# Windowed attention in six layers: probabilities divided ahead of their transposes, P V with V as weights, other order of the steps

## The chip, the cores and the metric

The kernel runs on one core of a Trainium2 chip. The metric is the device time of one execution in microseconds (us); runs of the same kernel are compared by their median. The core has five engines that each work through an instruction stream of their own, in order, and wait for one another by semaphores: TensorE (PE: matmuls from SBUF into PSUM), VectorE (DVE), ScalarE (ACT), GpSimd (POOL), and SyncE (SP), which here issues all DMA transfers.

## What is computed

The input is 2048 tokens of 128 numbers. After a layer norm two branches are added to it. One is a small linear attention, done once at the start. The other, nearly all of the time, has six layers of

```
q, k, v = split(shift_tokens(x) @ Wqkv)            # 16 heads of 64
q, k    = l2norm(q) * q_scale, l2norm(k) * k_scale, then rotary (xPos)
sim     = 8 q k^T for windows of 32 queries x 64 keys (own window and the one before), masked
out     = softmax(sim) v
x       = out @ Wo + x
x       = (a * gelu(gate)) @ W2 + b2 + x           # a, gate = layernorm(shift_tokens(x)) * g + b, times W1, plus b1
```

all in float32.

## The kernel before

**Tiling.** A step is 256 tokens (`T`) of one layer, two chunks (`C`) of 128; eight steps (`G`) are a layer, so there are 48 (`N`). Work of a step has three stages: `a_` (projections, squares of the norms, rotary), `b_` (attention, first half of Wo), `c_` (second half of Wo, layer norm, feed-forward). In iteration `it` the kernel does stage `a` of step `it`, `b` of step `it-1` and `c` of step `it-2` (`LAG`).

**Order.** `SCHEDULE` (line 57) is one list of small parts, written out by hand or by a planner. `run` (line 72) goes through it once an iteration, and each engine picks out the parts that it has a function for. So the list gives each engine's order; between engines only semaphores count. PE's order before is: `a_v0 c_wo a_v1 c_mu b_rqt a_x0 a_y0 c_var b_s0 a_x1 a_y1 b_s1 a_norm0 a_norm1 c_h0 a_x2 b_pt0 b_att0 a_y2 b_pt1 c_h1 a_sp0 a_norm2 b_ot0 a_sp1 c_h2 b_att1 c_down a_x3 a_y3 b_wo b_ot1 a_norm3`. DVE's is: `b_rcq c_xb b_rq c_zc a_mx0 a_my0 c_zn b_scale0 a_mx1 b_max0 c_zl b_scale1 a_rck b_max1 a_my1 b_sum0 a_mx2 b_div0 c_hm0 a_my2 a_kn0 c_hm1 b_sum1 c_hm2 a_kn1 b_div1 c_fin a_mx3 a_my3 b_xb`. POOL's is `a_rot0 b_sub0 b_sub1 a_rl a_rot1 a_halo w_l0 c_wl a_xl+1 a_rot2 a_rot3 w_l1 w_l2`.

**The parts that matter here**, for a chunk `c` of step `n`:

- `b_s` (line 497): a mask matmul into PSUM banks 2 and 3, then 64 (72 in the first chunk) small products of 64 x 32 queries as weights and 64 keys streamed, one for each head and window, in a tile of 64 rows x 32 columns of the PE array. A float32 matmul is two records in the trace, each with its weight load.
- `b_scale` (DVE, 770): PSUM times the inverse norm of q into `E`. `b_max`, `b_sub` (POOL, 1097), `b_exp` (ACT): maximum, subtraction, exponential, all in `E` (128 x 1024). `b_sum` (784): sum and reciprocal `ri`.
- `b_pt` (529): eight PE transposes of `E` into banks 4 and 5; `b_pto` (ACT) copies them to `PT`.
- `b_att` (537): 64 products with 32 columns of `PT` as weights and 64 of V (`V2`) streamed, into banks 2 and 3. `b_div` (790, line 795) multiplies by `ri` into `On`. `b_ot` (556) transposes `On` by PE into banks 4 and 5, `b_oto` (ACT) copies that to `OT`, `out_proj` (564: `b_wo`, `c_wo`) multiplies by Wo.
- `a_x`, `a_y`: six matmuls each of the projections of k and q (`ps<-xh,wh` and the like); `a_v`: six of v. `a_mx`, `a_my` (line 716): two multiplications each by the rotary tables; `a_rot` (POOL, 1090) adds them; `a_kn` (759) scales k by its inverse norm, `a_sp` is the matmul that spreads that norm.
- `c_mu`, `c_zc`, `c_zsq`, `c_var`, `c_rs`, `c_zn` (825), `c_zh`, `c_zl` (830): the layer norm of the feed-forward; `c_h`, `c_gelu`, `c_hm` (837), `c_down`: its matmuls and gate. `c_h1` waits for `c_hm0`, `c_h2` for `c_hm1`.

**Transfers.** SP issues them in one fixed order a step: `windows` (16 transfers of V from `Vs` into `V2`, line 271), `keys` (8, line 294, after `a_kn1`), `queries` (8, line 306, after `a_rot3`), `halo` (2, line 285), and the rotary table of the next step. `b_s0` of a step waits for its keys and queries.

Line 353 is the helper `mm`, line 525 the transposes, line 863 the helper `act`.

## Time and profile before

| what | us |
|---|---|
| median of 3 runs | 2080.44 (2080.12 to 2084.45) |
| the profiled execution | 2084.09 |
| its span, first to last instruction | 2081.5 |
| PE busy | 1759.1 (85%) |
| DVE busy | 1416.7 (68%) |
| ACT busy | 1124.9 (54%) |
| POOL busy | 801.3 (38%) |
| mean granted clock of TensorE | 0.929 of full speed |

"Busy" counts the time in which at least one instruction of the engine runs; matmuls overlap one another, so a busy PE isn't necessarily at its peak, and the mean time of one record is longer than the distance between two. An idle time is put down to what ended it: "issue" means that the profile shows nothing that the engine waited for.

### The profile page before, as it was taken

To read this page: it belongs to the slowest core of one execution; us is meant where nothing else is said; L and a number is where in the kernel's file an instruction comes from. 1 tells how busy PE (TensorE), PEld (TensorE's weight loads), DVE (VectorE), ACT (ScalarE), POOL (GpSimd) and SP (SyncE) were. 2 spreads that over 40 slices of the span, in tenths; PEclk is the share of its full clock that TensorE was granted. 3 is DMA by queue.
4 is the path that set the end of the run, shared out by engine and by line. 5 is a ranking of instruction groups with operands and counts; after the bars stand their busy time and mean duration, and the time that the engine had idled before them with its cause. 6 is when DMAs were issued, how large, how long until landed. Compare 5 with 4: busy or idle time off the path is not lost.

```text
span 2081.5 us, 81277 instructions
## 1 busy us (share of the span) xinstructions
PE 1759.1 (85%) x35952; PEld 1447.0 (70%) x35952; DVE 1416.7 (68%) x2130; ACT 1124.9 (54%) x2065; POOL 801.3 (38%) x612
## 2 busy tenths in 40 slices
...
GB/s 92 0 185 108 133 144 101 103 155 157 108 144 126 93 133 176 117 129 138 100 124 154 144 105 132 134 93 133 120 156 105 124 145 113 107 127 141 111 127 23
DMA packets 98318, 252.96 MB, mean 122 GB/s; under 512 B 29872, under 2 KB 36144, under 8 KB 97200
## 3 DMA queue, kind: packets, MB, share of 16 engines
...
## 4 chain that ended last, share of the span: by engine, by line
PE 51%; SPq 22%; DVE 10%; issue 9%; DMA 3%; POOL 3%; ACT 2%; DVEq 0%; ACTq 0%
PE ps L353 45%; SPq L314 6%; SPq L278 6%; PE ps L525 6%; SPq L281 5%; DVE UV L716 4%; POOL Qtb L1090 3%; SPq L303 2%; DVE On L795 2%; DMA V<-Vs 1%; ACT PT L863 1%; SPq L291 1%; DMA Qtb<-Qtb 1%; SPq L283 1%; DVE sq L697 1%
## 5 line engine op out<-in xcount | busy, mean ns | idle before, releaser
L716 DVE SCALAR_TENSOR_TENSOR UV<-ps,veca,rope 128x512 f32<-128x512 f32 x768 | 527.3, 738 | 55.1 <-PE ps L353 29.7
L863 ACT ACTIVATE sq<-ps 128x512 f32<-128x512 f32 (+1 forms) x400 | 227.5, 582 | 354.9 <-PE ps L353 341.9
L1090 POOL TENSOR_TENSOR Kt<-UV 128x512 f32<-128x512 f32 x192 | 250.1, 1325 | 423.2 <-DVE UV L716 423.2
L1090 POOL TENSOR_TENSOR Qtb<-UV 128x512 f32<-128x512 f32 x192 | 241.9, 1283 | 252.6 <-DVE UV L716 252.5
L1100 POOL TENSOR_TENSOR E<-E,mx 128x1024 f32<-128x1024 f32 x96 | 190.2, 1982 | 319.4 <-DVE mx L782 319.4
L353 PE MATMUL ps<-Kb,Qtb 64*32 64x64 f32 (+1 forms) x12288 | 187.5, 236 | 87.9 <-issue 87.6
L353 PE MATMUL ps<-xh,wh 128*128 128x256 f32 x768 | 250.0, 326 | 12.3 <-ACT sq L863 4.2
L353 PEld LDWEIGHTS ps<-Kb,Qtb 64*32 64x32 f32 x12288 | 161.0, 112 | 121.8 <-issue 121.4
L353 PE MATMUL ps<-xh,wl 128*128 128x256 f32 x768 | 226.5, 295 | 4.1 <-issue 4.1
L353 PE MATMUL ps<-xl,wh 128*128 128x256 f32 x768 | 226.7, 295 | 2.3 <-issue 2.3
L353 PE MATMUL ps<-V,PT 64*32 64x64 f32 x12288 | 154.2, 229 | 48.3 <-issue 48.2
L776 DVE TENSOR_TENSOR E<-ps,rq 128x1024 f32<-128x1024 f32 x96 | 117.3, 1222 | 111.8 <-PE ps L353 111.6
L353 PE MATMUL ps<-OT,wo 128*128 128x128 f32 x1536 | 187.1, 275 | 0.6 <-issue 0.6
L353 PEld LDWEIGHTS ps<-OT,wo 128*128 128x128 f32 x1536 | 182.9, 192 | 5.5 <-issue 1.4
L353 PE MATMUL ps<-sq,ind 128*32 128x256 f32 x1536 | 169.0, 411 | 8.6 <-issue 7.3
L353 PEld LDWEIGHTS ps<-xh,wh 128*128 128x128 f32 x768 | 154.3, 201 | 26.0 <-issue 6.9
L353 PEld LDWEIGHTS ps<-V,PT 64*32 64x32 f32 x12288 | 132.1, 106 | 56.0 <-issue 53.7
L353 PEld LDWEIGHTS ps<-xh,wl 128*128 128x128 f32 x768 | 155.8, 203 | 7.1 <-issue 5.9
L863 ACT ACTIVATE E<-E 128x1024 f32<-128x1024 f32 x96 | 101.5, 1058 | 105.9 <-POOL E L1100 105.8
L353 PEld LDWEIGHTS ps<-xl,wh 128*128 128x128 f32 x768 | 156.1, 203 | 2.2 <-issue 2.2
L795 DVE TENSOR_TENSOR On<-ps,ri 128x1024 f32<-128x1024 f32 x96 | 116.8, 1217 | 57.3 <-issue 49.6
L863 ACT ACTIVATE hid<-ps,vecc 128x256 f32<-128x256 f32 x144 | 69.0, 479 | 139.8 <-PE ps L353 138.8
...
## 6 DMA issues: line engine op xcount, KB each, us to landing
...
```

The costliest lines, as they stand in the source:

```text
L278: e.dma_start(V2[r * DH + W:(r + 1) * DH, m % 2, C * w:C * w + C, :], Vs[w * W:(w + 1) * W, r, :, :]).then_inc(s["v2_in"], 16)
L281: e.dma_start(V2[r * DH:r * DH + W, m % 2, C * w + C:C * w + 2 * C, :], Vs[w * W:(w + 1) * W, r, :, :]).then_inc(s["v2_in"], 16)
L303: e.dma_start(Kb[p0:p0 + W, j0:j0 + HQ, :], Kt[hq * W:(hq + 1) * W, half, :, :]).then_inc(s["k_in"], 16)
L314: e.dma_start(Qb[p0:p0 + W, j0:j0 + HQ, :], Qt[hq * W:(hq + 1) * W, half, :, :]).then_inc(s["q_in"], 16)
L353: return e.matmul(out, lhsT, rhs, start=start, stop=stop, **kw)
L525: ins = e.transpose(ps[:, 4 + h // 4, (h % 4) * P:(h % 4 + 1) * P], src[:, h, :, :], ident[:, :])
L716: e.scalar_tensor_tensor(UV[:, p % 2, slot, :].rearrange("p (i t) -> p i t", i=2), ps[:, half, :].rearrange("p (i t) -> p i t", i=2), veca ...
L776: e.tensor_tensor(E[:, c].rearrange("p j r k -> p r j k"), ps[:, 2:4, :].rearrange("p r (j k) -> p r j k", k=KEYS), by_row.unsqueeze(3).br ...
L795: e.tensor_tensor(On[:, :, :, :].rearrange("p j r k -> p r j k"), ps[:, 2:4, :].rearrange("p r (j k) -> p r j k", k=DH), ri[:, c].rearrang ...
L863: return e.activation(out, in_, f, **kw)
L1090: e.tensor_tensor(dst, u, v, op).then_inc(s["rot_done"], 1)
L1100: e.tensor_tensor(ev, ev, mx[:, c].unsqueeze(2).broadcast_to([P, H, KEYS]), ALU.subtract).then_inc(s["sub_done"], 1)
```

## The change

Four things are changed.

1. The probabilities are divided by their sum ahead of the transposes: `b_div` (which read PSUM) goes, `b_nrm` multiplies `E` by `ri`, in SBUF, in place; `b_pt` waits for it.
2. P V is formed with V as weights (64 x 64) and 32 columns of `PT` streamed, in tiles of 64 x 64 of the array. The result comes out transposed as Wo needs it, so `b_ot` and `On` go; `b_oto` copies banks 2 and 3 to `OT`, and the host lays Wo out otherwise.
3. `b_s` and `b_att` become four parts each, of four head pairs. Centering in the layer norm is done by the matmul (`cen` = identity minus the mean), so `c_zc` goes, and `c_zsq` and `c_zn` read PSUM.
4. The list has another order, and waits for a layer's weights are made once a layer. `windows` now waits for the halo of the step before.

PE's order after is: `a_v0 a_v1 a_x0 a_y0 c_wo b_rqt a_x1 b_s0 b_s1 a_y1 c_mu c_var b_s2 b_s3 a_norm0 a_norm1 a_x2 a_y2 c_h0 b_pt0 c_h1 b_att0 a_norm2 c_h2 a_sp0 b_pt1 b_att1 a_sp1 c_down a_x3 a_y3 b_att2 b_wo b_att3 a_norm3`. DVE's is: `b_rcq a_mx0 a_my0 c_xb b_rq a_mx1 b_scale0 a_my1 b_max0 c_zn b_scale1 b_max1 a_rck c_zl b_sum0 b_nrm0 a_mx2 c_hm0 b_sum1 c_hm1 b_nrm1 a_my2 c_hm2 a_kn0 a_kn1 c_fin a_mx3 a_my3 b_xb`. POOL's is `a_xl+1 a_rot0 b_sub0 b_sub1 a_rot1 a_rl w_l0 a_rot2 w_l1 a_halo a_rot3 w_l2 c_wl`.

```diff
-SCHEDULE = """b_lnq b_rcq a_vs0 c_xs c_xb b_rq a_vs1 a_v0 c_zc a_rot0 c_zsq c_wo a_mx0 a_sqy0 a_v1 c_rs c_mu b_rqt a_x0
...
+SCHEDULE = """b_rcq a_v0 a_mx0 a_vs0 a_my0 a_v1 c_xb a_vs1 a_x0 b_lnq a_xs+1 a_y0 b_rq a_sqy0 a_sqx0 a_xh+1 c_xs c_wo a_xl+1
+    b_rqt w_h0 a_x1 a_mx1 a_rot0 a_sqy1 b_scale0 b_s0 b_sub0 c_zsq c_rs b_sub1 a_my1 b_max0 b_s1 a_y1 c_mu a_rot1
+    c_zh c_var a_sqx1 b_s2 b_s3 w_h1 c_zn b_exp0 b_scale1 a_rl w_l0 b_max1 a_rck a_lnk a_norm0 a_sqy2 b_exp1
+    a_norm1 a_x2 a_y2 c_h0 c_gelu0 b_pt0 c_zl a_rot2 c_h1 b_pto0 b_att0 a_sqx2 b_sum0 c_gelu1 a_rh a_norm2 c_h2
+    a_sp0 b_pt1 b_att1 c_gelu2 w_l1 a_sp1 b_nrm0 a_mx2 b_oto0 c_down c_hm0 a_halo a_rot3 b_sum1 c_hm1 b_nrm1 a_x3
+    b_pto1 a_my2 c_hm2 a_kn0 a_sqy3 c_wh a_y3 b_att2 a_sqx3 w_l2 a_kn1 c_fin b_wo a_mx3 b_att3 a_my3 a_norm3 c_wl
+    w_h2 b_xb b_oto1""".split()
...
@@ -271,6 +271,8 @@
             def windows(m):
 
                 e.wait_ge(s["vs_done"], m * 4 + 4)
+                if m:
+                    e.wait_ge(s["v2_halo"], m * 32)
...
@@ -494,21 +497,23 @@
-            def b_s(n, c):
-
-                if c == 0:
+            def b_s(n, i):
+
+                c, heads = i // 2, range(i % 2 * HQ, i % 2 * HQ + HQ)
+                chosen = 0 if n % G == 0 and c == 0 else 1
+                if i % 2 == 0:
+                    if i == 2:
+                        e.wait_ge(s["e_done"], n * C + c)
+                    elif n:
+                        e.wait_ge(s["ots_done"], n * 4)
+                    for r in range(2):
+                        if i == 0 and r == 1:
+                            e.wait_ge(s["k_in"], n * 128 + 128)
+                        mm(ps[:, 2 + r, :].rearrange("p (j k) -> p j k", j=HP), identb[:, :],
+                           mask[:, chosen:chosen + 1, :].broadcast_to([P, HP, KEYS]), True, False, skip_group_check=True)
+                if i == 0:
                     e.wait_ge(s["q_in"], n * 128 + 128)
...
             def b_pt(n, c):
-                e.wait_ge(s["p_done"], n * C + c + 1)
+                e.wait_ge(s["pn_done"], n * C + c + 1)
...
+            def b_att(n, i):
+
+                c, heads = i // 2, range(i % 2 * HQ, i % 2 * HQ + HQ)
+                if i == 0:
+                    e.wait_ge(s["e_done"], n * C + C)
+                elif i == 2:
+                    e.wait_ge(s["ots_done"], n * 4 + 2)
+                if i % 2 == 0:
+                    mm(ps[:, 2, 0:1], identb[:, :], identb[:, 0:1])
+                    e.wait_ge(s["pts_done"], n * 4 + 2 * c + 2)
+                for h in heads[::2]:
+                    for w in range(NW):
+                        for r, h in ((0, h), (1, h + 1), (0, h + 1), (1, h)):
+                            rows = slice(r * DH, (r + 1) * DH)
+                            ins = mm(ps[h % 2 * DH:(h % 2 + 1) * DH, 2 + r, h // 2 * P + w * W:h // 2 * P + (w + 1) * W],
+                                     V2[rows, n % 2, C * w + c, h * DH:(h + 1) * DH], PT[rows, h, w * W:(w + 1) * W],
+                                     tile_position=(r * DH, h % 2 * DH))
...
-                mm(ps[:, 2, 0:1], identb[:, :], identb[:, 0:1])
-                for h in range(HP):
-                    for r in range(2):
-                        for w in range(NW):
-                            rows = slice(r * DH, (r + 1) * DH)
-                            ins = mm(ps[w * W:(w + 1) * W, 2 + r, h * DH:(h + 1) * DH], PT[rows, h, w * W:(w + 1) * W],
-                                     V2[rows, n % 2, C * w + c, h * DH:(h + 1) * DH], tile_position=(r * DH, w * W))
-                ins.then_inc(s["o_done"], 1)
...
-                transposed(On[:, :, :, :], "ot_done")
...
             def c_mu(j, _):
                 e.wait_ge(s["z_act"], j * 2 + 2)
-                mm(ps[:, FF, 0:T], mean[:, :], zs[:, :]).then_inc(s["mu_done"], 1)
+                mm(ps[:, FF, 0:T], cen[:, :], zs[:, :]).then_inc(s["mu_done"], 1)
...
-            def b_div(n, c):
+            def b_nrm(n, c):
                 e.wait_ge(s["ri_done"], n * C + c + 1)
...
+                e.tensor_tensor(heads(E[:, c]), heads(E[:, c]), ri[:, c].unsqueeze(2).broadcast_to([P, H, KEYS]),
+                                ALU.mult).then_inc(s["pn_done"], 1)
...
-                e.scalar_tensor_tensor(zs[:, :], zs[:, :], vecc[:, j // G % 2, LG:LG + 1], zr[:, :], ALU.mult,
+                e.scalar_tensor_tensor(zs[:, :], ps[:, FF, 0:T], vecc[:, j // G % 2, LG:LG + 1], zr[:, :], ALU.mult,
...
-                    act(OT[:, 4 * i:4 * i + 4, :], ps[:, 4 + i, :]).then_inc(s["ots_done"], 1)
+                    act(OT[:, 4 * i:4 * i + 4, :], ps[:, 2 + i, :]).then_inc(s["ots_done"], 1)
...
-                act(zq[:, :], zs[:, :], ACT.Square).then_inc(s["zsq_done"], 1)
+                e.wait_ge(s["mu_done"], j + 1)
+                act(zq[:, :], ps[:, FF, 0:T], ACT.Square).then_inc(s["zsq_done"], 1)
```

## Rows read from the trace of the kernel before

**Rows 1.** The page, chain that ended last, by engine (q: its queue).
```profile
PE 51%; SPq 22%; DVE 10%; issue 9%; DMA 3%; POOL 3%; ACT 2%; DVEq 0%; ACTq 0%
```

**Rows 2.** Busy time and instructions by engine in the stretch of all steps.
```profile
core 0: us, PE busy (x) PEld busy (x) DVE busy (x) ACT busy (x) POOL busy (x), PEclk, DMA share, GB/s
143.00:2024.50 1881.50, 1639.07 (x34920) 1360.03 (x34920) 1301.55 (x1895) 1076.96 (x1972) 773.76 (x588) 0.95 0.55 127
```

**Rows 3.** Timeline of PE (start, us, engine, line, tiles, idle before): masks of `b_s0`.
```profile
143.03 0.99 PE L353 MATMUL ps<-mask,identb 128*128 128x512 bf16 x2 [2.83 <-DMA Qtb<-Qtb]
...
1552.23 0.61 PE L353 MATMUL ps<-mask,identb 128*128 128x512 bf16 x2 [1.01 <-DMA Qtb<-Qtb]
...
1588.75 0.59 PE L353 MATMUL ps<-mask,identb 128*128 128x512 bf16 x2
...
2024.54 1.03 PE L353 MATMUL ps<-mask,identb 128*128 128x512 bf16 x2 [1.28 <-DMA Qtb<-Qtb]
```

**Rows 4.** Timeline of SP's queue: keys and queries of one step.
```profile
1574.66 6.13 SPq L303 DMA_DIRECT2D Kb<-Kt  x8
1581.88 4.96 SPq L314 DMA_DIRECT2D Qtb<-Qtb  x8
```

**Rows 5.** Timeline of DVE in that step: `b_scale1`, `c_hm0`, `a_kn1`.
```profile
1559.45 1.23 DVE L776 TENSOR_TENSOR E<-ps,rq 128x1024 f32<-128x1024 f32 x1 [0.58 <-PE ps L353]
...
1567.15 0.47 DVE L837 SCALAR_TENSOR_TENSOR hid<-ps,vecc,hid 128x256 f32<-128x256 f32 x1
...
1573.42 1.21 DVE L759 TENSOR_TENSOR Kt<-ps,Kt 128x1024 f32<-128x1024 f32 x1
```

**Rows 6.** The page, groups: busy us, mean ns of one, idle before and releaser.
```profile
L353 PE MATMUL ps<-Kb,Qtb 64*32 64x64 f32 (+1 forms) x12288 | 187.5, 236 | 87.9 <-issue 87.6
...
L353 PE MATMUL ps<-V,PT 64*32 64x64 f32 x12288 | 154.2, 229 | 48.3 <-issue 48.2
...
L353 PEld LDWEIGHTS ps<-OT,wo 128*128 128x128 f32 x1536 | 182.9, 192 | 5.5 <-issue 1.4
...
L353 PEld LDWEIGHTS ps<-V,PT 64*32 64x32 f32 x12288 | 132.1, 106 | 56.0 <-issue 53.7
```

**Rows 7.** Groups of instructions kept apart by shape.
```profile
L525 PE MATMUL ps<-ident,On 128*128 128x128 f32 x768 | 103.1, 278 | 0.0
...
L825 DVE SCALAR_TENSOR_TENSOR zs<-zs,vecc,zr 128x256 f32<-128x256 f32 x48 | 54.0, 1125 | 4.4 <-ACT zr L863 4.4
...
L353 PE MATMUL ps<-zs,mean 128*128 128x256 f32 x96 | 33.6, 431 | 2.5 <-ACT zs L863 2.5
...
L863 ACT ACTIVATE hid<-zs 128x256 f32<-128x256 f32 x48 | 20.0, 418 | 23.5 <-DVE zs L820 23.5
```

**Rows 8.** DMA queues in the stretch of all steps: packets, MB, share.
```profile
q8 instruction: 276, 4.52, 1.1%
```

**Rows 9.** Timeline of PE behind a stall, and behind a Q K burst.
```profile
942.95 0.43 PE L353 MATMUL ps<-Kb,Qtb 64*32 64x64 f32 x6 [3.08 <-issue]
...
944.75 0.41 PE L353 MATMUL ps<-xh,wh 128*128 128x256 f32 x1
944.96 0.41 PE L353 MATMUL ps<-xh,wl 128*128 128x256 f32 x1
...
1554.60 0.39 PE L353 MATMUL ps<-xh,wh 128*128 128x256 f32 x1
1554.83 0.28 PE L353 MATMUL ps<-xh,wl 128*128 128x256 f32 x1
1554.94 0.28 PE L353 MATMUL ps<-xl,wh 128*128 128x256 f32 x1
```

**Rows 10.** Timelines of DVE and POOL where both read SBUF.
```profile
1552.86 1.16 DVE L825 SCALAR_TENSOR_TENSOR zs<-zs,vecc,zr 128x256 f32<-128x256 f32 x1
...
1552.45 2.71 POOL L1090 TENSOR_TENSOR Kt<-UV 128x512 f32<-128x512 f32 x2 [8.28 <-DVE UV L716]
1558.56 2.08 POOL L1100 TENSOR_TENSOR E<-E,mx 128x1024 f32<-128x1024 f32 x1 [3.40 <-DVE mx L782]
1562.22 1.90 POOL L1100 TENSOR_TENSOR E<-E,mx 128x1024 f32<-128x1024 f32 x1 [1.58 <-DVE mx L782]
```

100 lines of the change are left out of this document (36 added, 64 removed).

## The prediction

> **What bounds the kernel now.** I read the chain of work that ended last first: half of it is TensorE (PE), a fifth SP's queue [rows 1]. Over the 1881.5 us in which the steps run, PE is busy 87% of the time and VectorE (DVE) 69% [rows 2], so no engine alone is the answer. The kernel repeats one step 48 times. The PE timeline shows the mask matmul that opens `b_s0` at 143.03 and for the last time at 2024.54 [rows 3]: 47 periods of 40.03 us. What lies around them, 200 of the 2081.5 us, the diff hardly touches.
>
> A period has two parts. At the end of `a_kn1` (1573.42 + 1.21 = 1574.63 [rows 5]) SP begins to issue the eight key transfers (6.13 us), then the eight query transfers (4.96 us, from 1581.88) [rows 4], and the next `b_s0` starts at 1588.75 [rows 3]: 14.1 us, 1.1 of it a gap between keys and queries. Without that gap it would be 13.0; I take 13.6. Nothing in the diff shortens it, since `b_s0` still waits for all queries. The other part, **T, runs from the start of `b_s0` to the end of `a_kn1`**: 40.03 - 13.6 = 26.4 us in the mean, and 1574.63 - 1552.23 = 22.4 us in the step read here. Period = T + 13.6, as long as PE's own work in the second part is no longer than SP's. The question is what the change does to T.
>
> In that step T is: 7.2 us of PE up to `b_scale1` (1559.45), a gapless run of DVE of 8.2 us up to the end of `c_hm0` (1567.62), then 7.0 us of PE, one GELU, `c_hm2` and `a_kn1` [rows 5]. The mean T is 4.0 us longer. Most of that is idle PE that the profile calls "issue", inside bursts of small matmuls: 87.9 us in the Q K bursts and 48.3 us in the P V bursts [rows 6], 1.8 and 1.0 us a step. The queue named "instruction" made 276 transfers [rows 8] while PE carried out 34920 matmuls and as many weight loads [rows 2]: one for 253 instructions. A Q K burst of 144 matmuls and 144 loads ends 2.37 us after its mask started (1552.23 to 1554.60 [rows 3, 9]), so I read these stalls as PE running out of code. A second loss follows them: behind the 3.08 us stall that ended at 942.95 two neighbouring matmuls start 0.21 us apart (944.75, 944.96), against 0.11 at 1554.83 [rows 9]: half of the clock. The granted clock of the stretch is 0.95 [rows 2]: 1.2 in place of 2.4 GHz for a tenth of it, 188 us, so at most 94 us lost or 2 us a step.
>
> **The change, part by part, in us of T.**
>
> 1. *Transposes of the output (`b_ot`) gone.* 768 matmuls in two groups a step; 103.1 us of busy time in all [rows 7], so 1.07 a group. One group lies in T (counted in 4), the other where SP is the bound and it is worth nothing.
>
> 2. *P V with V as weights.* The number of matmuls stays. Each streams 32 columns instead of 64 and loads 64 weight columns instead of 32, on four tiles of the array instead of eight. No row shows such a load. Now a record takes 154.2 us / 12288 = 12.5 ns of PE. T holds two half bursts, 128 records. From below, half of the columns could be worth half of the time: -0.8. From above: a load 32 wide lasts 106 ns and one 128 wide 192 ns [rows 6], 0.9 ns a column, so one 64 wide some 29 ns more; if it doesn't hide, that over four tiles is 7 ns a record, +0.9. I take +0.1: columns times four tiles against columns times eight is the same work per tile, and what is nearest is the rate of now.
>
> 3. *Mean, square and variance moved.* `c_mu`, `c_zsq`, `c_var` now stand between the Q K bursts, where `a_x1` stood. Out: six matmuls 0.12 apart, 0.7 us. In, as a chain: a matmul pair (0.43), the square on ScalarE (0.42), a pair (0.43) [rows 7], and some 0.4 between engines: 1.65. Net +0.95.
>
> 4. *The run of DVE, and PE behind it.* `b_nrm0` takes the place of `b_div0`, same shape, same 1.2 us; `a_my1`, as many elements as `a_kn1` (1.2), moves ahead of `b_scale1`, where DVE waits for PE anyway; `c_zl` (0.4, as `c_hm0`) comes in: -0.8, of which a later GELU gives back 0.15. Net -0.65. Behind it PE loses `b_ot0` (1.0) and half of the second P V burst (0.8), but gets `b_pt1` (1.0) and waits for `b_nrm1`, in all 7.3 for 7.0: +0.3. PE will have to wait ahead of `b_pt0`, since sum and division now stand before the transpose; that wait is DVE's run seen from PE, not a cost of its own.
>
> 5. *Shorter bursts.* `b_att` is split with other work between, so 253 instructions last over 4 us there. P V stalls go: -1.0, and -0.2 at the transpose ahead. `b_s` is not broken up: in PE's order `b_s0 b_s1` and `b_s2 b_s3` are neighbours, a burst of 292 instructions as before. But the 1.65 us of slow work of 3 stand behind it, in which code arrives, and `windows` now waits for the halo's landing, so its transfers start about 1 us later. Of 1.8 I take 1.1 off; the bounds are 0 and 1.8.
>
> 6. *`c_zl` and `b_nrm` against GpSimd.* Both read two tiles of SBUF. So did `c_zn`: 1125 ns in the mean [rows 7], where `c_hm0`, same shape but one input in PSUM, takes 0.47 [rows 5]. At 1552.86 it took 1.16 beside GpSimd's `a_rot` (two in 2.71, from 1552.45): it ended about when the first of these did. The other way round, `b_sub0` at 1558.56, just behind `c_zl`, takes 2.08, `b_sub1` at 1562.22 only 1.90 [rows 10]. The one that comes second waits for the first. After the change `c_zl` stands 0.3 us behind the start of `b_sub1`: +1.4, with `b_sum0` queued behind it on DVE and `c_h0` on PE waiting for it. `b_nrm0` comes 1.4 us later, beside `a_rot1` (two of 1.3): 0 to +1.2, and I take 0, because it arrives near the border of the two. `c_zn` itself gets 0.67 shorter, where DVE waits for PE.
>
> 7. *Clock.* Fewer stalls (3.0 to 0.7 us a step), but a PE wait at `b_pt0`: -0.3 of the 2.
>
> 8. *At nothing.* The waits taken off (weights, once a layer) and Wo's other order are no work. `c_zc` goes off T. `a_v0 a_v1`, now neighbours, wait some 0.5 us for the copies to `Vs`, in SP's part: PE's work from `a_sp1` to `b_s0` adds up to 14.3 us and begins 1.2 before the end of `a_kn1`, so 13.1 against 13.6. With that cover gone it would cost up to 0.5. `windows`, 1 us later in SP's queue, ends long before `keys` must start.
>
> Sum: 0.1 + 0.95 - 0.65 + 0.3 - 1.2 - 1.1 + 1.4 - 0.3 = -0.5 a step; times 47, -24 us. The profiled execution took 2084.1 (span 2081.5); the median of the runs is 2080.4, and taken off that it gives **2057 us**.
>
> **Rivals.**
> (a) *DVE and GpSimd don't meet on the way.* Without the 1.4, and with 0.5 more of stall and clock gone: -2.4 a step, -113: **1968 us**. For it: these places are shown by one line only. Against it: the mean of `c_zn` leaves room for no more than a few short ones. Chance 0.27.
> (b) *Slower: `b_nrm0` is held up too.* Place: DVE ahead of `b_pt0`. Price +1.2, and PE idles near 3 us there, as long as in the stall of [rows 9] that half clock followed: +0.7. So -0.5 + 1.9 = +1.4, +66: **2146 us**. It decides once the delays ahead of `b_pt0` pass 1.4 + 0.5 = 1.9 us. Chance 0.20.
> The Trainium skill ("SBUF — State Buffer", who interferes with whom) says that a VectorE instruction with two SBUF inputs contends with a GpSimd instruction that reads SBUF, and that the later one blocks fully. By that rule `c_zl` and `b_nrm0` are both held, which is (b).
> (c) *The Q K stalls stay*, as these bursts are no shorter: +1.1, so +0.6 a step, +28: **2108 us**. Chance 0.11.
> The Trainium skill ("Runtime: NRT & Kernel Launch", instruction fetch mechanics) says that code comes in blocks of 256 instructions and that crossing into the next is mostly hidden. The block agrees with the 253; the hiding doesn't agree with the idle time inside the bursts.
>
> **Chances.** Forecast 0.42, (a) 0.27, (b) 0.20, (c) 0.11. The forecast itself has some 40 us on either side (2017 to 2097), so of its share 0.29 lies below, 0.07 at no change and 0.06 above. A measurement can tell 0.2% (4 us) from nothing. Faster 0.56, same 0.07, slower 0.37. The range runs from (a) nearly to (b): 1972 to 2138.
>
> **What would show it.** Mask to mask 39.5 us, and 13.6 from `a_kn1` to the mask; if the latter changes much, SP was not the bound. `c_zl` 1.9 us and `b_nrm0` 1.2 for the forecast; 0.5 and 1.2 for (a); 1.9 and 2.3 for (b). PE idle ahead of `b_pt0` for 1.5 to 2.5 us, released by DVE. "Issue" idle under 5 us for P V and near 35 for Q K; if it is near 90, (c). A P V half of about 0.75 us. A granted clock under 0.92 speaks for (b).

## The result, and the profile after

The changed kernel takes **2208.6 us** (median of 4 runs, 2192.7 to 2222.0) against 2080.3 us before: a ratio of 1.0617, 95% interval 1.0539 to 1.0695. The forecast was 2057 us with a range up to 2138, so sign and range are both wrong: the kernel became slower, by 62 us more than even rival (b) (2146 us) allowed. The profiled execution of after ran 2222.0 us.

The page of after: its span, busy time, and the chain that ended last. It answers [rows 1].

```profile
span 2220.1 us, 79013 instructions
...
PE 1865.9 (84%) x35184; PEld 1493.5 (67%) x35184; DVE 1512.9 (68%) x2083; ACT 1141.9 (51%) x2065; POOL 799.6 (36%) x612
...
PE 70%; DVE 17%; issue 7%; ACT 4%; DMA 1%; SPq 1%; POOL 0%; POOLq 0%; ACTq 0%; DVEq 0%
```

SP's queue had 22% of the chain before and has 1% now: the part that it bounded is bounded by TensorE. The mask matmuls that open the next step say the same: TensorE was idle ahead of them for 15.4 us before, mostly until the queries had landed, and for 0.6 us now (group of TensorE by shape):

```profile
L355 PE MATMUL ps<-mask,identb 128*128 128x512 bf16 x192 | 63.6, 415 | 0.6 <-DVE E L782 0.4 <-issue 0.2
```

VectorE went from 10% to 17%. The stretch of all steps answers [rows 2]: the granted clock of TensorE falls from 0.95 to 0.90. It has two levels, full (2.4 GHz) and half (1.2 GHz), so a mean of 0.90 is a fifth of the time at half clock.

```profile
core 0: us, PE busy (x) PEld busy (x) DVE busy (x) ACT busy (x) POOL busy (x), PEclk, DMA share, GB/s
141.60:2158.50 2016.90, 1745.81 (x34160) 1406.49 (x34159) 1397.27 (x1847) 1092.24 (x1966) 773.05 (x588) 0.90 0.50 118
```

The groups of the page answer [rows 6] (busy us, mean ns of one, idle before and its releaser):

```profile
L355 PE MATMUL ps<-PT,V 64*64 64x32 f32 x12288 | 241.9, 232 | 1.4 <-ACT PT L861 1.4
L355 PEld LDWEIGHTS ps<-PT,V 64*64 64x64 f32 x12288 | 220.0, 148 | 17.1 <-issue 8.2
L533 PE MATMUL ps<-ident,E 128*128 128x128 f32 x768 | 133.9, 332 | 107.6 <-DVE E L798 107.6
...
L355 PE MATMUL ps<-Kb,Qtb 64*32 64x64 f32 (+1 forms) x12288 | 180.8, 232 | 34.5 <-issue 34.2
...
L355 PE MATMUL ps<-zh,w1h 128*128 128x256 f32 (+1 forms) x288 | 116.8, 405 | 79.9 <-DVE zl L828 68.2
```

The stalls that the prediction wanted gone are gone: 48.3 to 1.4 us in P V, 87.9 to 34.5 in Q K. But P V costs 241.9 us of busy time, not 154.2, and TensorE now waits 107.6 us for `b_nrm` (L798) ahead of the transposes and 68.2 us for `c_zl` (L828).

The timelines of VectorE and GpSimd in the step that begins at 1084.83, from `b_scale1`'s end on:

```profile
1097.57 1.90 POOL L1099 TENSOR_TENSOR E<-E,mx 128x1024 f32<-128x1024 f32 x1 [2.28 <-DVE mx L788]
1097.73 2.01 DVE L828 SCALAR_TENSOR_TENSOR zl<-zs,vecc,zh 128x256 fp32r<-128x256 f32 x1
...
1099.42 2.69 POOL L1089 TENSOR_TENSOR Kt<-UV 128x512 f32<-128x512 f32 x2
...
1099.67 1.21 DVE L792 TENSOR_REDUCE rs<-E 128x16 f32<-128x1024 f32 x1
...
1101.20 2.00 DVE L798 TENSOR_TENSOR E<-E,ri 128x1024 f32<-128x1024 f32 x1
...
1107.56 1.76 DVE L798 TENSOR_TENSOR E<-E,ri 128x1024 f32<-128x1024 f32 x1
```

`c_zl`, 0.52 us in the mean where nothing holds it (run `both`), ends 0.3 us after `b_sub1` on GpSimd does; `b_sum0` (L792), with one SBUF input, isn't held beside `a_rot1`; `b_nrm0` is (2.00 instead of 1.2), and so is `b_nrm1`. The same stretch on TensorE (weight loads left out of the view by "..."):

```profile
1099.80 0.38 PE L355 MATMUL ps<-zh,w1h 128*128 128x256 f32 x1 [2.19 <-DVE zl L828]
...
1100.26 0.28 PE L355 MATMUL ps<-zh,w1h 128*128 128x256 f32 x1
...
1100.38 0.28 PE L355 MATMUL ps<-zh,w1l 128*128 128x256 f32 x1
...
1103.25 1.97 PE L533 MATMUL ps<-ident,E 128*128 128x128 f32 x8 [2.48 <-DVE E L798]
...
1105.77 0.41 PE L355 MATMUL ps<-zh,w1h 128*128 128x256 f32 x1
...
1105.99 0.41 PE L355 MATMUL ps<-zh,w1l 128*128 128x256 f32 x1
...
1106.57 1.68 PE L355 MATMUL ps<-PT,V 64*64 64x32 f32 x64
...
1111.39 1.14 PE L355 MATMUL ps<-PT,V 64*64 64x32 f32 x64
```

Two waits, 2.19 and 2.48 us, with 1.0 us of matmuls between them. Ahead of the second, neighbouring matmuls start 0.12 us apart; behind it 0.22, half clock, and half a P V burst takes 1.68 us instead of 1.14.

**All runs in one table.** I cut each of the 47 steps in four, by starts in the timelines of TensorE and VectorE: head (mask of `b_s0` to `b_scale1`), middle (to the first transpose of `b_pt0`), tail (to the end of `a_kn1`), and the second part (to the next mask). T is the first three. Each run has its own ratio to the kernel before on its chip, whose medians lie between 2075 and 2086 us; so where two runs of different chips are close, the ratios decide and not the times. `output changed` means that this part of the computation is not the reference's.

| kernel | median us | ratio (95%) | clock | head | middle | tail | second |
|---|---|---|---|---|---|---|---|
| before | 2080.3 | 1 | 0.929 | 9.14 | 3.15 | 14.02 | 13.73 |
| after | 2208.6 | 1.062 (1.054-1.070) | 0.893 | 8.66 | 8.27 | 11.97 | 14.01 |
| nrm_psum | 2180.8 | 1.046 (1.039-1.053) | 0.908 | 8.48 | 7.58 | 11.82 | 14.01 |
| zl_early | 2141.3 | 1.032 (1.022-1.042) | 0.906 | 8.67 | 6.10 | 12.40 | 14.04 |
| both | 2153.8 | 1.033 (1.026-1.039) | 0.904 | 8.48 | 6.05 | 12.62 | 14.03 |
| pv_old (output changed) | 2137.4 | 1.025 (1.021-1.030) | 0.896 | 8.84 | 8.30 | 10.73 | 13.49 |
| both_pvold (output changed) | 2063.8 | 0.991 (0.987-0.994) | 0.920 | 8.70 | 6.07 | 11.28 | 13.48 |
| stream64 (output changed) | 2203.9 | 1.059 (1.052-1.066) | 0.900 | 8.80 | 8.29 | 11.55 | 14.06 |
| after_fill | 2129.2 | 1.022 (1.019-1.026) | 0.963 | 8.51 | 8.61 | 9.84 | 14.03 |
| both_fill | 2068.4 | 0.994 (0.990-0.998) | - | - | - | - | - |
| both_fill2 | 2051.4 | 0.985 (0.982-0.987) | 0.964 | 8.65 | 6.21 | 10.57 | 14.03 |
| norm_early | 2169.4 | 1.046 (1.042-1.049) | 0.917 | 8.43 | 9.40 | 9.86 | 14.03 |
| norm_early_fill | 2204.0 | 1.062 (1.059-1.066) | 0.922 | 8.51 | 9.39 | 10.41 | 14.03 |
| b_att_split | 2126.2 | 1.022 (1.015-1.029) | 0.951 | 9.22 | 3.12 | 13.90 | 14.56 |
| b_both_split | 2147.8 | 1.033 (1.026-1.040) | 0.961 | 10.18 | 2.63 | 13.90 | 14.60 |
| b_att01 | 2083.9 | 1.001 (0.998-1.005) | 0.948 | 9.24 | 3.11 | 13.95 | 13.77 |
| b_fill | 2052.2 | 0.990 (0.987-0.992) | 0.941 | 8.93 | 3.36 | 13.29 | 13.69 |

(The profiled execution of both_fill was slower than its others, 2092.9 us, so only its time is used.)

Over all 47 tails together the granted clock is 0.93 before, 0.76 after, 0.80 in `both` and 1.00 in `after_fill`: the tail is where the changed kernel lost its clock.

### The profile page after: what moved, and what is told of

It is laid out like the page before. It is cut to its first block, busy times and chain, and to the rows that moved or that the text cites. A ratio compares the mean times of both kernels' runs of the same rounds, so it can differ in the third digit from the quotient of the medians.

```text
span 2220.1 us, 79013 instructions
## 1 busy us (share of the span) xinstructions
PE 1865.9 (84%) x35184; PEld 1493.5 (67%) x35184; DVE 1512.9 (68%) x2083; ACT 1141.9 (51%) x2065; POOL 799.6 (36%) x612
## 4 chain that ended last, share of the span: by engine, by line
PE 70%; DVE 17%; issue 7%; ACT 4%; DMA 1%; SPq 1%; POOL 0%; POOLq 0%; ACTq 0%; DVEq 0%
PE ps L355 65%; PE ps L533 4%; DVE zl L828 4%; DVE E L798 3%; DVE E L782 2%; DVE rs L792 2%; ACT Vs L861 1%; ACT sq L861 1%; DVE UV L721 1%; DVE R L750 1%; ACT hid L861 1%; DVE sq L702 1%; SPq L305 1%; DVE ri L794 1%; PE ps L497 0%
## 5 line engine op out<-in xcount | busy, mean ns | idle before, releaser
L721 DVE SCALAR_TENSOR_TENSOR UV<-ps,veca,rope 128x512 f32<-128x512 f32 x768 | 535.5, 744 | 249.1 <-PE ps L355 201.4
L1099 POOL TENSOR_TENSOR E<-E,mx 128x1024 f32<-128x1024 f32 x96 | 182.9, 1905 | 325.3 <-DVE mx L788 325.3
L355 PE MATMUL ps<-PT,V 64*64 64x32 f32 x12288 | 241.9, 232 | 1.4 <-ACT PT L861 1.4
L355 PEld LDWEIGHTS ps<-PT,V 64*64 64x64 f32 x12288 | 220.0, 148 | 17.1 <-issue 8.2
L533 PE MATMUL ps<-ident,E 128*128 128x128 f32 x768 | 133.9, 332 | 107.6 <-DVE E L798 107.6
L355 PE MATMUL ps<-sq,ind 128*32 128x256 f32 x1536 | 208.8, 435 | 15.7 <-issue 12.3
L355 PE MATMUL ps<-Kb,Qtb 64*32 64x64 f32 (+1 forms) x12288 | 180.8, 232 | 34.5 <-issue 34.2
L861 ACT ACTIVATE OT<-ps 128x512 f32<-128x512 f32 x192 | 104.2, 594 | 169.8 <-PE ps L355 169.8
L533 PEld LDWEIGHTS ps<-ident,E 128*128 128x128 f32 x768 | 109.4, 170 | 117.5 <-DVE E L798 117.5
L1069 POOL TENSOR_TENSOR xl<-xs,xh 128x256 fp32r<-128x256 f32 x48 | 35.8, 746 | 417.8 <-ACT xh L861 417.8
L355 PE MATMUL ps<-zh,w1h 128*128 128x256 f32 (+1 forms) x288 | 116.8, 405 | 79.9 <-DVE zl L828 68.2
```

What stands on the lines that cost most here:

```text
L355: return e.matmul(out, lhsT, rhs, start=start, stop=stop, **kw)
L533: ins = e.transpose(ps[:, 4 + h // 4, (h % 4) * P:(h % 4 + 1) * P], src[:, h, :, :], ident[:, :])
L721: e.scalar_tensor_tensor(UV[:, p % 2, slot, :].rearrange("p (i t) -> p i t", i=2), ps[:, half, :].rearrange("p (i t) -> p i t", i=2), veca ...
L861: return e.activation(out, in_, f, **kw)
L1069: e.tensor_tensor(xl[:, m % 2, :], xs[:, :], xh[:, m % 2, :], ALU.subtract).then_inc(s["xl_done"], 1)
L1099: e.tensor_tensor(ev, ev, mx[:, c].unsqueeze(2).broadcast_to([P, H, KEYS]), ALU.subtract).then_inc(s["sub_done"], 1)
```

## The experiments

The theory after reading the traces was rival (b) of the prediction plus two things: the new form of P V is dearer on TensorE, and the waits bring half clock for the work behind them.

**1. The two holds by GpSimd.** `nrm_psum` writes the reciprocals to PSUM, so that `b_nrm` has one SBUF input:

```diff
-                e.reciprocal(ri[:, c], rs[:, c]).then_inc(s["ri_done"], 1)
+                if n or c:
+                    e.wait_ge(s["pts_done"], n * 4 + 2 * c)
+                e.reciprocal(ps[:, 4, 0:H], rs[:, c]).then_inc(s["ri_done"], 1)
...
-                e.tensor_tensor(heads(E[:, c]), heads(E[:, c]), ri[:, c].unsqueeze(2).broadcast_to([P, H, KEYS]),
+                e.tensor_tensor(heads(E[:, c]), heads(E[:, c]), ps[:, 4, 0:H].unsqueeze(2).broadcast_to([P, H, KEYS]),
```

`zl_early` moves `c_zl` in the order (the lines are pieces of `SCHEDULE`, here and below), and `both` has the two edits:

```diff
-b_scale1 a_rl w_l0 b_max1 a_rck
+b_scale1 a_rl w_l0 c_zl b_max1 a_rck
...
-b_pt0 c_zl a_rot2
+b_pt0 a_rot2
```

> The changed kernel with one edit: the reciprocal of the sums is written to PSUM (bank 4) and `b_nrm` reads it there, so that it has one input in SBUF instead of two. In the changed kernel `b_nrm` takes 1.75 to 2.0 us, in the kernel before `b_div` took 1.21. Theory H (an operation of VectorE with two inputs in SBUF is held up by a GpSimd operation that reads SBUF): `b_nrm` takes 1.21 us, the TensorE wait ahead of `b_pt0` gets 0.8 us shorter, and the second `b_nrm` gives another 0 to 0.5: 40 to 60 us off the 2209. Rival R (the step is as long as TensorE's own work and VectorE's delay is hidden): `b_nrm` gets shorter, the time does not move. Rival M (in-place SBUF multiplication is slow of itself): `b_nrm` stays at 1.75 or more.

> The changed kernel with one edit in the order: `c_zl` stands ahead of `b_max1` on VectorE, so before `b_sub1` can start on GpSimd. Theory H: `c_zl` takes 0.47 us in place of 2.0, `c_h0` no longer waits 2.2 us, `b_sum0` starts some 1.6 us earlier relative to the end of `b_max1`; but `b_nrm0` then arrives while both halves of `a_rot1` still run and may wait longer, up to 2.4 us, so that 0.5 to 1.5 us a step are left: 25 to 70 us off. Rival R (VectorE's delay is hidden): no change. Theory C (the two waits of TensorE, 2.2 us at `c_h0` and 2.5 us at `b_pt0`, with 0.8 us of work between them, lead to the stretch at half clock behind them): without the first wait the granted clock of the stretch rises from 0.89 towards 0.93.

> The changed kernel with both edits: the reciprocal in PSUM, and `c_zl` ahead of `b_max1`. Theory H: no VectorE operation between `b_max1` and `b_pt0` is held up; the stretch from the end of `b_max1` to the end of `b_nrm0` falls from 5.7 to 3.1 us, and with `b_nrm1` some 2.4 to 3.0 us a step are won, 110 to 140 us: 2070 to 2100. With theory C another 20 to 40 us by the clock. Rival R: no change. If the sum of the two single edits is much less than this, the second delay had only moved to the other place.

Groups of VectorE by shape, first of `nrm_psum`, then of `both`:

```profile
L800 DVE TENSOR_TENSOR E<-E,ps 128x1024 f32<-128x1024 f32 x96 | 116.7, 1215 | 1.7
...
L830 DVE SCALAR_TENSOR_TENSOR zl<-zs,vecc,zh 128x256 fp32r<-128x256 f32 x48 | 88.5, 1843 | 0.6 <-ACT zh L863 0.6
```

```profile
L799 DVE TENSOR_TENSOR E<-E,ps 128x1024 f32<-128x1024 f32 x96 | 116.7, 1216 | 1.7
...
L829 DVE SCALAR_TENSOR_TENSOR zl<-zs,vecc,zh 128x256 fp32r<-128x256 f32 x48 | 24.9, 518 | 0.6 <-ACT zh L862 0.6
```

After has 1843 ns for `b_nrm` (176.9 us over 96) and 1824 for `c_zl`. Taking the second SBUF input away ends the hold of `b_nrm`, and only that; moving `c_zl` ends its own. It also shortens `b_nrm0`, with both inputs still in SBUF, from 1.94 to 1.33 us in the mean, while `b_nrm1` stays at 1.74: so working in place in SBUF isn't slow of itself. The middle shrinks from 8.27 to 6.05 us: the holds are worth 2.2 us a step there. But the times give 28, 67 and 55 us: `nrm_psum` is short of the 40 to 60 expected, `both` gives half of its 110 to 140 and is not better than `zl_early` alone, which lies at the upper end of its range. The tail says why: it grew by 0.65. Timelines of `both`, VectorE, then TensorE, then pieces of its chain of waits (start, us, what):

```profile
1109.33 1.22 DVE L787 TENSOR_REDUCE mx<-E 128x16 f32<-128x1024 f32 x1
...
1110.79 1.21 DVE L791 TENSOR_REDUCE rs<-E 128x16 f32<-128x1024 f32 x1
1112.03 0.26 DVE L795 RECIPROCAL ps<-rs 128x16 f32<-128x16 f32 x1
1112.33 1.22 DVE L799 TENSOR_TENSOR E<-E,ps 128x1024 f32<-128x1024 f32 x1
```

```profile
1113.61 1.09 PE L532 MATMUL ps<-ident,E 128*128 128x128 f32 x8 [2.50 <-DVE E L799]
1115.97 0.58 PE L354 MATMUL ps<-zh,w1h 128*128 128x256 f32 x1 [1.27 <-DVE hid L836]
1116.35 0.42 PE L354 MATMUL ps<-zh,w1l 128*128 128x256 f32 x1
1116.57 0.41 PE L354 MATMUL ps<-zl,w1h 128*128 128x256 f32 x1
```

```profile
1110.62 1.91 POOL E L1100
...
1113.63 1.28 ACT L862
...
1114.93 0.48 ACT hid L862
...
1115.43 0.49 DVE hid L836
```

VectorE runs without a gap or a hold, and TensorE still waits 2.50 us for it: maximum, sum, reciprocal and product stand in front of the transpose now. A second wait of 1.27 us follows, and its chain is another: GpSimd's `b_sub1`, the exponential, ScalarE's table load (1.28 us) and the GELU. Behind both the matmuls stand 0.22 apart: half clock.

The Trainium skill ("SBUF — State Buffer", the section on who interferes with whom) says that a VectorE instruction with two SBUF inputs contends with a GpSimd instruction that reads SBUF and that the later one blocks fully. The trace agrees: in the mean `c_zl` takes 0.52 us away from GpSimd's `b_sub1` and 1.82 beside it, and `b_nrm` 1.22 with one SBUF input and 1.84 with two.

**2. What the clock costs.** `after_fill` is the changed kernel with dummy matmuls (identity times identity, 512 bf16 columns), whose result nobody reads, put ahead of the two waits; nothing else moves.

```diff
             def b_pt(n, c):
-                e.wait_ge(s["pn_done"], n * C + c + 1)
...
+                if c == 0:
+                    for _ in range(9):
+                        mm(ps[:, 5, :].rearrange("p (j k) -> p j k", j=4), identb[:, :],
+                           identb[:, :].unsqueeze(1).broadcast_to([P, 4, P]))
+                e.wait_ge(s["pn_done"], n * C + c + 1)
```

(and eight ahead of `zl_done` in `c_h0`.) `both_fill` has 24 of 128 columns ahead of `b_pt0` on top of `both`; `both_fill2` has six of 512 there and five behind the transposes, ahead of `c_h1`.

> The changed kernel with the reciprocal in PSUM and c_zl early (as in the run of both edits, 2153.8 us, clock 0.904), and 24 dummy matmuls of 128 bf16 columns (about 1.3 us at full clock) on TensorE ahead of the wait of b_pt0 for the normalised probabilities (mean idle there about 1.55 us a step). They add work that nobody needs. Theory C, that wait is what brings TensorE to half clock for the next 6 to 7 us of the step (about 2 us a step): with the wait filled the granted clock rises above 0.93 and the time falls by 47 x 1 to 2 us, to 2060 to 2107 us, though there is more work. Rival N, the clock follows from something else (the wait at c_h1 behind it, or the kind of work): clock stays about 0.90 and the time stays at 2154 or rises by up to 60 us.

> The changed kernel, nothing moved, with dummy matmuls of 512 bf16 columns on TensorE ahead of its two long waits: eight (about 1.7 us at full clock) ahead of c_h0's wait for zl (2.2 us) and nine (about 1.9 us) ahead of b_pt0's wait for the normalised probabilities (2.5 us). VectorE and GpSimd work as before, so the waits end no earlier. Theory C, much of what the change lost is half clock after these waits: granted clock 0.95 or more (0.893 without), and 47 steps x 1.5 to 2.5 us less than 2208.6, so 2091 to 2138 us. Rival, the lost time is VectorE's and GpSimd's and the clock is a symptom: clock up, time within 20 us of 2209.

> Both edits (reciprocal in PSUM, c_zl early) with six dummy matmuls of 512 bf16 columns ahead of b_pt0's wait (about as long as the 24 of 128 columns of the run both_fill, which was 2068.4 us, clock 0.943, and in 18 fewer instructions) and five (1.1 us) behind its transposes, where c_h1 waits 1.3 us for the hidden layer. Theory C: steps at full clock take 37.9 us in both_fill (some 20 of 47), the others fall to half clock behind an instruction stall and the remaining wait of 1.3 us; with that filled too, clock 0.96 or more and 2010 to 2050 us. If the remaining wait does nothing to the clock, 2055 to 2080 us.

The timeline of TensorE in a step of `after_fill`, and two of its steps, mask to mask, in windows (columns as above); then the window of the step of after shown above:

```profile
1225.31 2.12 PE L355 MATMUL ps<-identb 128*128 128x512 bf16 x9
1227.73 1.09 PE L533 MATMUL ps<-ident,E 128*128 128x128 f32 x8 [0.31 <-DVE E L806]
1229.44 0.38 PE L355 MATMUL ps<-zh,w1h 128*128 128x256 f32 x1 [0.62 <-DVE hid L843]
...
1230.37 1.14 PE L355 MATMUL ps<-PT,V 64*64 64x32 f32 x64
```

```profile
1212.24:1251.86 39.62, 38.10 (x748) 29.45 (x746) 30.01 (x42) 23.04 (x42) 15.40 (x13) 1.00 0.60 135
1377.22:1416.88 39.66, 38.18 (x748) 29.65 (x746) 29.70 (x42) 25.88 (x45) 23.44 (x16) 1.00 0.51 121
```

```profile
1084.83:1128.65 43.82, 36.81 (x731) 30.11 (x729) 30.21 (x42) 26.01 (x45) 23.45 (x16) 0.88 0.48 111
```

816 useless matmuls (17 a step, some 0.21 us apart, about 170 us of TensorE) make the kernel 79 us **faster**. The holds are as long as before (the middle even grows, 8.27 to 8.61 us), the tail falls by 2.1 us, and 30 of the 47 steps run at clock 1.00 throughout, where none of after's do. The issue idle of the Q K group is 34.2 us in both, so it isn't the instruction supply that gained. Half clock behind the waits thus costs this kernel 79 us or more. That is not yet its share of the 128 us lost to the kernel before, which has half clock too (the control below). On top of `both` the same means is worth 85 us (`both_fill`) and 102 us (`both_fill2`); the latter, at 2051.4 us, beats the kernel before by 1.5%. Its steps at clock 1.00 take some 38 us (31 of 47):

```profile
1299.30:1337.17 37.87, 36.72 (x741) 28.73 (x740) 27.28 (x41) 22.93 (x42) 15.22 (x13) 1.00 0.57 135
...
1412.86:1458.94 46.08, 37.65 (x741) 29.51 (x739) 27.29 (x42) 23.59 (x43) 16.83 (x14) 0.93 0.61 154
```

Slow ones, as the second, have stalls in their Q K bursts that the profile calls issue (36.0 us over the run).

The control is `b_fill`: three such matmuls in the kernel before, where TensorE waits 0.83 us for the copies of the transposed probabilities.

> The kernel before with three dummy matmuls of 512 bf16 columns (0.64 us at full clock) on TensorE between the first transposes of the probabilities and the first P V burst, where TensorE waits 0.83 us for ScalarE's copies in most steps. It is the control for the runs with dummy matmuls: is half clock behind short waits a cost that any such kernel has, or one of the changed kernel's long waits? If the long waits of 2 us and more make the difference: 2084 us within 10, clock 0.929 to 0.94. If any filled wait pays: clock 0.95 or more and 2050 us or less, and then the runs with dummies say little of the change.

2052.2 us, 1.0% faster than before: near the second case, though the clock is only 0.941 (0.929 in the profile of before). Issue idle fell too, from 87.6 to 74.9 us in Q K and from 48.2 to 34.7 in P V, so how much of its 23 us is clock isn't settled. It does limit what may be said. Filled waits help the kernel before as well, and with both kernels filled the repaired change brings next to nothing: each against before on its own chip, the ratios are 0.985 and 0.990. And of the 79 us only what goes beyond the kernel before's own loss is a loss by the change: 79 - 23 = 56 us by these two fillings. By the traces it is at most 94 us: a step of after has 8.4 us at half clock, one of before 4.4, and if TensorE had set the pace in all of it the other 4.0 us would have cost 2.0.

**3. P V.** `pv_old` takes P V of the changed kernel back to the old form (PT as 32-wide weights, 64 columns of V streamed); `stream64` keeps the new weights and streams 64 columns instead of 32.

```diff
-                for h in heads[::2]:
-                    for w in range(NW):
-                        for r, h in ((0, h), (1, h + 1), (0, h + 1), (1, h)):
+                for h in heads:
+                    for r in range(2):
+                        for w in range(NW):
                             rows = slice(r * DH, (r + 1) * DH)
-                            ins = mm(ps[h % 2 * DH:(h % 2 + 1) * DH, 2 + r, h // 2 * P + w * W:h // 2 * P + (w + 1) * W],
-                                     V2[rows, n % 2, C * w + c, h * DH:(h + 1) * DH], PT[rows, h, w * W:(w + 1) * W],
-                                     tile_position=(r * DH, h % 2 * DH))
+                            ins = mm(ps[w * W:(w + 1) * W, 2 + r, h * DH:(h + 1) * DH], PT[rows, h, w * W:(w + 1) * W],
+                                     V2[rows, n % 2, C * w + c, h * DH:(h + 1) * DH], tile_position=(r * DH, w * W))
```

> The changed kernel with the P V matmuls in the form of before (32 columns of PT as weights, 64 of V streamed, eight tiles of the array), in the same two halves a chunk; all else as changed, so what is copied to OT is laid out otherwise and the output is not the reference's. The changed form costs TensorE 241.9 us for 12288 records, 19.7 ns each, the one before 154.2 us, 12.5 ns. Theory P (64 weight columns on a quarter of the array are dear): a half burst falls from 1.06 to 0.75 us, four a step, 1.2 us a step or 56 us, and up to 1.5 of that where the clock is halved: 55 to 90 us off. Rival R2 (these bursts lie where something else is waited for): under 20 us.

> The changed kernel with the right operand of each P V matmul widened from 32 columns (one window of PT) to 64 (two windows); weights (64x64 tiles of V), number of matmuls and their order are kept, so the output is not the reference's. It asks what the 19.7 ns of a record in the changed form consist of (16.6 ns at full clock, against 12.5 and 11 ns in the form before). Theory L, the 64x64 weight loads set the pace and the streamed columns lie beside them: no change, 2209 us within 10, and a record stays at 19.7 ns. Theory S, load and stream are served one after the other: 32 more columns at 2.4 GHz are 13.3 ns a matmul over 4 matmuls at work on four quadrants, 3.3 ns a record at least, up to 13.3 ns if nothing overlaps; 12288 records then cost 41 to 163 us more, part of it also at half clock: 2250 to 2370 us, with records of 23 to 33 ns.

> Both edits together with P V in its old form (PT as 32-wide weights, 64 streamed columns of V) in the changed halves; the output is not the reference's, since nothing transposes it back. Alone, the old form gave 71 us and both edits 55. If they are three separate costs, 2137 - 55 = about 2082 us, which is the kernel before (2080): the form of P V, the two holds and the clock behind them are then all of the loss. If the clock ties them together, less is left to gain (2105 to 2125 us). Second part of a step 13.5 us in either case.

Half a burst (64 matmuls) at full clock, in the timelines of TensorE of `pv_old` and of `stream64`; after has 1.14 us above:

```profile
1128.59 0.86 PE L355 MATMUL ps<-V,PT 64*32 64x64 f32 x64
```

```profile
1114.40 1.16 PE L355 MATMUL ps<-PT,V 64*64 64x64 f32 x64
```

Twice the streamed columns cost nothing (1.16 to 1.14, and 2204 to 2209 us): the streamed columns don't set the pace. What does isn't settled: the forms differ in the columns of a load (64 against 32) and in the number of tiles that work side by side (four against eight), and no run changes one without the other. The new form costs 0.28 us more per half burst, four of them a step: 1.1 us, of which 0.56 lie in T. `pv_old` gains 71 us, some 20 more than 47 times 1.1; the tail holds the rest (1.24 us shorter; its time at half clock falls from 5.9 to 4.6 us a step, worth up to 0.65). The second part falls from 14.0 to 13.5 us. With the holds gone too (`both_pvold`) the kernel is at 2063.8 us, below the 2082 of three separate costs and 0.9% below the kernel before: order, bursts and the missing output transposes, which the old form would need, are a small gain together, and P V's form, the holds and what the clock does with them are the whole loss.

The Trainium skill ("TensorE: Matmul & The Clock Gate", LDWEIGHTS) says that a load takes its columns divided by 1.2 in ns, whatever the rows: 53 ns for 64. An estimate by it, with loads on the four tiles side by side, is 13.3 ns a matmul; in the trace the matmuls of a half burst start 14.5 ns apart (1.14 us less the last one's 0.23, over 63). For the old form the same estimate is 27 ns over eight tiles, 3.3 ns, and the trace has 10.2 ns. So the rule comes near for the new form alone and doesn't explain what the old one costs.

**4. Are the stalls that the change removed worth their time?** In the kernel before, the bursts alone were cut in two, nothing else: `b_att_split` (both P V bursts), `b_att01` (the first only), `b_both_split` (P V and Q K).

```diff
-b_sum0 a_y2 a_mx2
+b_sum0 a_y2 b_att1 a_mx2
...
-c_hm2 b_att1 c_down a_x3
+c_hm2 b_att2 c_down b_att3 a_x3
```

> The kernel before, with each P V burst (256 instructions of the form before) cut into two of four head pairs in TensorE's order: the second half of the first head half behind the down projection's neighbour a_y2, that of the second behind c_down; nothing else moved, nothing in another form. If the idle time of 48.3 us with the releaser issue in the P V group (about 1.0 us a step) comes from bursts longer than the instruction supply carries (theory F), it goes to under 10 us and a step becomes up to 1.0 us shorter where PE sets the end of the first part: 2080 - 47 x 0.5 to 1.0 = 2033 to 2057 us. If those stalls are something else (PSUM, DMA of V), the idle time stays and the time too, 2080 within 6.

> The kernel before, with the bursts of P V and of Q K both cut into parts of four head pairs and other TensorE work between the parts (P V as in b_att_split; Q K: first half, q chunk transposes a_x1, second half; then a_y1, first half, a_norm0, second half, a_norm1). Theory F: both issue groups (87.9 us Q K, 48.3 us P V) mostly go, 1.9 + 1.0 us a step at the most; the Q K part saved lies on the way of b_sub0 only where PE is later than VectorE: I expect 2000 to 2045 us, the best of all kernels so far. Rival: the second half of the scores comes later for GpSimd (b_sub1) and VectorE is then held longer behind it, so that nothing is gained over b_att_split.

> The kernel before with only the first of its two P V bursts cut in two (the second half of it behind a_y2), the second left whole; in b_att_split the second part of a step grew from 13.7 to 14.6 us because the end of the second burst stood behind c_down, and the first part stayed at 26.2 us. Theory F (instruction supply stalls are time on the path of the first part): issue idle of the P V group 48.3 -> about 30 us, first part 0.3 to 0.6 us shorter, 2052 to 2068 us. Rival (the first part ends with VectorE's and GpSimd's work, and stalls of TensorE there are hidden): first part 26.2 to 26.4 us and 2080 us within 8.

Groups of TensorE in `b_att_split`, by shape:

```profile
L352 PE MATMUL ps<-V,PT 64*32 64x64 f32 x12288 | 169.8, 225 | 21.5 <-issue 21.4
...
L352 PE MATMUL ps<-zh,w1h 128*128 128x256 f32 x192 | 68.0, 354 | 40.8 <-DVE hid L838 32.7 <-issue 5.5 <-DVE zl L831 2.6
```

27 us of P V stall went away, the clock rose to 0.951, and T stayed: 26.24 us against 26.31. So neither the idle time nor the better clock was worth anything there. Most of the saved idle time is found again ahead of `c_h1`, where the wait for `hid` rose to 32.7 us from 11.1. The stalls stood where TensorE was early anyhow. `b_att01` takes away only 7 us (P V issue idle 41.0, where 30 was expected), so it adds little on this; T is 26.30, the second part stays at 13.77, and the time at 2084 us. `b_both_split` cut the Q K stalls from 87.6 to 33.6 us of issue idle and lost more, where 2000 to 2045 us were expected: its head is 1.0 us longer. Its edit puts `a_x1` inside the first Q K burst, on which VectorE and GpSimd wait; that this is the cause is argued, not shown. The second part of both splits is 0.8 to 0.9 us longer: the last half of P V stands behind `c_down` there, and in `b_att01`, where it doesn't, the part has its old length. All three are splits of the kernel before; what the stalls were worth in the changed kernel's order no run shows.

**5. Needed work in place of dummies.** `norm_early` moves `a_norm2` ahead of `b_pt0`, and `a_sqx2`, which feeds it, ahead of `b_exp1`, in the kernel `both`.

```diff
-a_sqy2 b_exp1 a_norm1 a_x2 a_y2 c_h0 c_gelu0 b_pt0
+a_sqy2 a_sqx2 b_exp1 a_norm1 a_x2 a_y2 c_h0 c_gelu0 a_norm2 b_pt0
...
-b_att0 a_sqx2 b_sum0 c_gelu1 a_rh a_norm2 c_h2
+b_att0 b_sum0 c_gelu1 a_rh c_h2
```

> Both edits (reciprocal in PSUM, c_zl early; 2153.8 us, clock 0.904, 41.2 us a step) and, in place of dummies, work that is needed anyway: a_norm2 (eight matmuls, 1.06 us at full clock) moved ahead of b_pt0, with a_sqx2 that feeds it ahead of b_exp1 on ScalarE. The wait at b_pt0 (1.55 us a step) becomes about 0.5, the one at c_h1 grows to about 1.9 us. Theory C with the work at its real place: b_pt0's wait is filled and 1.06 us of work leaves the part behind it, 1 to 2.5 us a step: 2035 to 2107 us. Rival: the wait at c_h1 (1.9 us) now brings half clock by itself: 2110 to 2150 us.

> The kernel norm_early with five dummy matmuls (1.1 us) ahead of c_h1's wait, as in both_fill2 (2051.4 us, clock 0.964, steps of 37.8 us at full clock), but without its six dummies ahead of b_pt0. If TensorE sets the end of the part, 1.0 to 1.28 us a step of dummy work is gone: 37.8 -> about 36.8 us in steps at full clock, 1990 to 2010 us. If VectorE and ScalarE set it (chain to the hidden layer), no more than both_fill2: 2051 within 10.

Both missed, and the timelines of VectorE, ScalarE and TensorE tell why at once:

```profile
1122.36 1.22 DVE L799 TENSOR_TENSOR E<-E,ps 128x1024 f32<-128x1024 f32 x1
1123.50 1.40 DVE L720 SCALAR_TENSOR_TENSOR UV<-ps,veca,rope 128x512 f32<-128x512 f32 x2
...
1124.94 0.60 ACT L862 ACTIVATE sq<-ps 128x512 f32<-128x512 f32 x1 [2.55 <-DVE UV L720]
...
1125.59 1.92 PE L354 MATMUL ps<-sq,ind 128*32 128x256 f32 x8 [4.46 <-ACT sq L862]
```

The square waits for rotary products that stand behind `b_nrm0` on VectorE, and TensorE, which works in order, waits for the square: 4.46 us in place of 2.5, at half clock behind: the eight transposes take 1.77 us, not 1.09. `norm_early_fill` shows that filling a wait doesn't pay of itself: its five dummies made the kernel slower, 2204.0 us against 2169.4, with nearly the same clock (0.922 against 0.917). I had looked at what TensorE had left to do, not at when its inputs come. Whether another order fills this wait with needed work stays open.

## Why the prediction was wrong, by its own steps

- **What held.** The period's two parts; where the waits would stand (for `b_pt0`, 1.5 to 2.5 us, released by VectorE: 2.48 measured in the step shown); the hold of `c_zl` by `b_sub1` (forecast 1.9 us, measured 1.82); P V's stalls under 5 us and Q K's near 35. The clock of 0.893 is the mark that the prediction had named for (b), and `b_nrm0` of 2.0 us is nearer to its 2.3 than to the forecast's 1.2. But (b) gave 2146 us: it priced the hold and not P V, the stalls or most of the clock. The half burst of P V (0.75 us expected, 1.14 measured) and the part from `a_kn1` to the mask (13.6 and 14.0) missed their marks.
- **Step 6 failed on `b_nrm`.** It was put at nothing "because it arrives near the border". Both `b_nrm` are held (1843 ns in the mean against 1215), the first for the most part because `c_zl`'s hold shifts it onto `a_rot1`: with `c_zl` early, without any edit to it, `b_nrm0` falls from 1.94 to 1.33 us and `b_nrm1` stays (the mean of the two is 1536 ns then). Holds in the middle: 2.2 us, not 1.4.
- **Step 7 failed, in sign and most of all.** I took 0.3 us off a step for a faster clock. Half clock takes 79 us or more in all, 1.7 a step and over, and 1.2 to 2.0 a step more than in the kernel before. (b) had priced it at 0.7. The two waits stand 1.0 us apart, and what follows them is TensorE's heaviest stretch of the tail.
- **Step 2 was mis-sized.** +0.1 us of T, measured +0.56 at full clock, between it and the upper bound (+0.9). The argument "columns times four tiles against columns times eight" counted streamed columns, and these cost nothing.
- **Step 8 failed, in part from the same cause.** TensorE's work in the second part was put at 13.1 us against SP's 13.6. The part takes 14.0 us now and TensorE is hardly idle in it: TensorE bounds it, +0.3 us a step. With P V's old form, two half bursts of 0.28 us less each, it is 13.5.
- **Step 5 was right on the idle time and wrong on its worth.** In P V -1.2 us a step was credited; in the kernel before, cutting only the bursts took 0.6 us of stall off a step and left T where it was. For Q K, the head fell by 0.5 us, with step 3 in it: the shortest heads, which have no stall, are 6.74 before and 7.07 after, so step 3 costs about 0.3 and not 0.95, and the stalls gave 0.8 of the 1.1 credited.
- **Step 4's sentence that the wait at `b_pt0` is "not a cost of its own"** left out what it does to the clock, and what it does in the second wait behind it (`c_h1`).

The sum again. For middle and tail the steps gave -0.35 us; measured is +3.07 (8.27 + 11.97 against 3.15 + 14.02). The four misses there, holds +0.8, clock +1.5 to 2.3 (1.2 to 2.0 lost instead of 0.3 gained), P V +0.5 and its stalls +1.2, add up to 4.0 to 4.8 and not to 3.4. They are not independent: `pv_old` shortens the tail by 1.24 us where P V alone is 0.56, the rest being about what its shorter time at half clock is worth. How the loss divides between them exactly stays open. The head is 0.5 shorter (forecast 0.15), the second part 0.3 longer (forecast 0). In all 2.9 x 47 = 135 us of the 138.6 between the two spans.
